# A four-layer graph network on one core: other preparation, other order of work, the edge maximum subtracted on TensorE and the sums inverted on ScalarE

## The reference, cut to what matters

```python
m     = segment_max(logits, dst)                 # one maximum for each target and head
ex    = exp(logits - m[dst])
denom = segment_sum(ex, dst)
out   = segment_sum(x_src_projected * (ex / denom[dst]), dst)
```

## Time and profile before

| what | us |
|---|---|
| median of 3 runs (4057.2 to 4076.98) | 4066.97 |
| the profiled execution, its own time | 4061.93 |
| the profiled execution, span of its instructions | 4060.2 |
| `prepare` | 0 to 68 |
| `node_pass` | 68 to 1232 |
| pass "0" and `source_columns` | 1232 to 1836 |
| pass "1" | 1836 to 2397 |
| pass "2a" | 2397 to 2945 |
| pass "2b" | 2945 to 3470 |
| pass "3" | 3470 to 4060.2 |

### The profile page before, as it was taken

The page is one execution under the profiler, slowest core; times in us unless marked ns, Lnnn a source line. Parts: engine busy times, 40 slices in busy tenths (PEclk is TensorE's granted clock), DMA queues, the critical chain, the costliest instruction groups (busy, mean ns, idle before and its releaser), DMA issues. The chain is left out here.

```text
span 4060.2 us, 72393 instructions
## 1 busy us (share of the span) xinstructions
PE 3500.2 (86%) x19961; PEld 2510.3 (62%) x20169; DVE 3558.8 (88%) x6756; ACT 2879.2 (71%) x9715; POOL 2308.0 (57%) x2305
## 2 busy tenths in 40 slices
PE   2999999999987999986999969999867777687775
PEld 2888888888864777764666645555534444354443
DVE  3899999999986999976999959999979999698786
ACT  2999999999975888875988855555546766344343
POOL 1577777777766777754433323345153442687777
PEclk9999999999988999998999989999989999898888
DMA  1455555555544343324544425555345554454442
GB/s 49 129 149 152 151 152 150 152 152 150 152 140 110 103 105 100 102 61 121 129 126 125 119 75 134 139 137 136 95 127 146 143 147 127 129 133 119 114 117 67
DMA packets 719120, 503.45 MB, mean 124 GB/s; under 512 B 141745, under 2 KB 621335, under 8 KB 718960
## 3 DMA queue, kind: packets, MB, share of 16 engines
q1 hardware_dynamic: 533072, 362.39, 33.0%
q0 software_dynamic: 56528, 81.64, 7.6%
q10 hardware_dynamic: 129360, 57.82, 5.1%
HBM read 304.28 MB, written 200.10 MB: 124 GB/s over the span
## 5 line engine op out<-in xcount | busy, mean ns | idle before, releaser
L1169 POOL DMA_INDIRECT slot_src_rows<-x,src_table_cols x392 | 420.7, 1073 | 453.1 <-PE psum L226 227.4
L237 ACT ACTIVATE node_z<-psum 128x128 f32<-128x128 f32 x1568 | 419.8, 325 | 22.5 <-PE psum L217 14.7
L1169 POOL DMA_INDIRECT slot2a_src_rows<-x,src_table_cols x196 | 220.5, 1125 | 335.0 <-PE psum L226 201.3
L646 ACT ACT_TABLE_LOAD x306 | 392.6, 1283 | 12.9 <-issue 7.7
L237 ACT ACTIVATION_READ_ACCUMULATOR node_z<-psum 128x1 f32 x1568 | 348.5, 227 | 0.0
L237 ACT ACTIVATE slot_logit<-psum 128x128 f32<-128x128 f32 x980 | 256.8, 279 | 125.9 <-PE psum L1337 99.8
L1169 POOL DMA_INDIRECT slot2b_src_rows<-xl,src_table_cols x196 | 198.2, 1011 | 257.1 <-PE psum L226 210.5
L1194 POOL DMA_INDIRECT out_nodes<-slot_new,out_index x196 | 243.0, 1240 | 59.8 <-issue 58.9
L1001 POOL DMA_INDIRECT node_gathered<-in_x,src_cols x196 | 235.8, 1203 | 47.0 <-issue 47.0
L1173 POOL DMA_INDIRECT slot_dst_rows<-in_x,dst_gather_cols x196 | 211.0, 1076 | 84.4 <-issue 50.9
L1166 POOL DMA_INDIRECT map_cols<-slot_map,src_cols x196 | 213.6, 1090 | 59.7 <-issue 59.7
(11 more groups left out here) (417 smaller groups left out, 12180.5 us busy)
## 6 DMA issues: line engine op xcount, KB each, us to landing
x<-node_x SPq DMA_DIRECT2D x294, 256.0 KB, 2.9
slot_neg<-neg SPq DMA_DIRECT2D x147, 256.0 KB, 4.5
node_xT<-in_x_T SPq DMA_DIRECT2D x98, 256.0 KB, 3.1
out_nodes<-node_x SPq DMA_DIRECT2D x98, 256.0 KB, 2.8
x<-slot_new ACTq DMA_DIRECT2D x98, 256.0 KB, 2.3
slot_keep<-keep SPq DMA_DIRECT2D x98, 256.0 KB, 4.2
slot_dst_rows<-x SPq DMA_DIRECT2D x98, 256.0 KB, 5.4
xl<-node_xl SPq DMA_DIRECT2D x98, 128.0 KB, 2.9
```

The lines of the kernel that those rows point to most:

```text
L237: ins = act.activation(g.z[u][:, t, :], rows[:, t, :], ACT.Square, scale=float(D ** -0.5), accum_out=sums[u][:, t:t + 1])
L646: act.add_instruction(mybir.InstLoadActFuncSet(name=nc.get_next_instruction_name(), ins=[], outs=[], act_func_set_id=wanted[0]))
L1169: pool.indirect_dma_start(src_rows[u][:, t, 0:src_width], None, table, column(c.src_table_cols[order], u, i, t))\
```

## The change

It touches `prepare`, `pe_rows`, the chains and steps of passes "0", "1", "2a" and "2b", the lookups of `slot_map`, and all five lists of `PLAN`.

- **`prepare`**: 60 loads in place of 62, in three groups with semaphores of their own, 33 issued by SyncE and 27 by ScalarE; work starts as its group arrives. The bias parts are made from columns by two small matmuls and one copy, where each was made from rows in 36 copies and 12 subtractions. After the wait for the last group VectorE has 39 instructions.
- **`pe_rows`**: the bias matmul reads 15 partitions (`level_of`, `bias_levels`), over the same columns.
- **"0", "1", "2a"**: `tot`, `rec`, `rs` and `rB` go. ScalarE takes the logarithm (`ln`) and the exponential of its negative (`inv`) of the whole 128x512 tile of sums in SBUF, and `agg` reads that. In "1" and "2a" VectorE first adds the two parts of the sum (`tot`, 128x512).
- **"1", "2a", "2b"**: `e_p` moves to TensorE, which adds `-I` times `fmax` to the logits in PSUM; ScalarE's `exp` is parted in `exp_p` (from PSUM) and `exp` (SBUF), 128x512 each.
- **"2a" and "2b"**: the leaky ReLU is made of a ReLU and a linear part, each with its own product, so VectorE's `z` goes. In "2a" the values are copied to `val` by ScalarE (`v`), which `pv` reads.
- **Lookups**: pass "0" makes 116 of the 196 (three for a chunk), pass "1" the others, two for a chunk; `source_columns` comes after "1".
- **`PLAN`**: new start times for every edge pass, on the same period; the lists of numbers are left out here.

```diff
 def pe_rows(pe, g, u, bank, parts, bias=None, width=P):
-        pe.matmul(bank(u)[:, 0:TILES * width], g.c.ones[:, 0:P], bias[:, 0:TILES * width], start=True, stop=False)
+        levels = tiles_of(g.c.bias_levels[:, :])[:, :, 0:width]
+        pe.matmul(bank(u)[:, 0:TILES * width].rearrange("p (t n) -> p t n", t=TILES), g.c.level_of[:, ROW_BIASES.index(bias), :], levels,
+                  start=True, stop=False)
...
+    by_sp = loads["rows"] + loads["first"][0::2] + loads["late"][0::2]
+    by_act = loads["first"][1::2] + loads["late"][1::2]
...
+        @block.scalar
+        def _(act):
+            with nc.allow_non_contiguous_dma("a few vectors"):
+                for item in by_act:
+                    act.dma_start(*item).then_inc(arrived[group_of[id(item)]], 16)
...
-        "2a": [("DVE", "dst"), ("PE", "z"), ("PE", "zo"), ("ACT", "z"), ("ACT", "zo"), ("DVE", "z"),
-               ("PE", "r"), ("PE", "v")],
-        "2b": [("DVE", "dst"), ("PE", "z"), ("ACT", "z"), ("DVE", "z"), ("PE", "r")],
+        "2a": [("PE", "v"), ("ACT", "v"), ("DVE", "dst"), ("PE", "z"), ("PE", "zo"), ("ACT", "z"), ("ACT", "zo"),
+               ("PE", "r"), ("PE", "o")],
+        "2b": [("DVE", "dst"), ("PE", "z"), ("ACT", "z"), ("ACT", "zl"), ("PE", "r")],
...
     softmax = [("DVE", "fc"), ("DVE", "f"), ("DVE", "shift"), ("DVE", "e_p"), ("DVE", "e_c"), ("ACT", "exp")]
+    if layer in ("1", "2a", "2b"):
+        softmax = [("DVE", "fc"), ("DVE", "f"), ("PE", "e_p"), ("DVE", "shift"), ("DVE", "e_c"), ("ACT", "exp_p"), ("ACT", "exp")]
     if layer == "0":
-        sums = [("DVE", "v"), ("DVE", "den"), ("DVE", "pv"), ("PE", "tot"), ("DVE", "num"), ("DVE", "tot")]
+        sums = [("DVE", "v"), ("DVE", "den"), ("DVE", "pv"), ("ACT", "ln"), ("DVE", "num"), ("ACT", "inv"), ("DVE", "agg")]
     elif layer == "1":
-        sums = [("ACT", "exps"), ("PE", "o"), ("DVE", "den"), ("DVE", "pv"), ("PE", "tot"), ("DVE", "num"), ("DVE", "sv"), ("DVE", "ns"), ("DVE", "tot")]
+        sums = [("ACT", "exps"), ("PE", "o"), ("DVE", "den"), ("DVE", "pv"), ("DVE", "num"), ("DVE", "sv"), ("DVE", "tot"), ("ACT", "ln"),
+                ("DVE", "ns"), ("ACT", "inv"), ("DVE", "agg")]
...
     mean = [("DVE", "rec")] + ([] if layer == "2b" else [("ACT", "rs")]) + [("PE", "rB"), ("DVE", "agg")]
+    if layer in ("0", "1", "2a"):
+        mean = []
...
     if layer == "0":
-        side += [("POOL", f"dst_gather{t}") for t in range(TILES)]
+        side = [("POOL", f"gather{t}") for t in range(3)] + [("POOL", f"dst_gather{t}") for t in range(TILES)]
+    elif layer == "1":
+        side += [("POOL", "gather_row0"), ("POOL", "gather_row1")]
...
+                elif step == "exp_p":
+                    act.wait_ge(*g.PE.done(u, i, "e_p"))
+                    act_copy(act, g, u, expo[u][:, 0, :], (A if layer == "2a" else B)(u), ACT.Exp)
+                elif step == "exp" and layer in ("1", "2a", "2b"):
+                    act.wait_ge(*g.DVE.done(u, i, "e_c"))
+                    act_copy(act, g, u, expo[u][:, 1, :], expo[u][:, 1, :], ACT.Exp)
...
+                elif step == "ln" and layer in ("1", "2a"):
+                    act.wait_ge(*g.DVE.done(u, i, "tot"))
+                    act_copy(act, g, u, expo[u][:, 2, :], expo[u][:, 2, :], ACT.Ln)
+                elif step == "ln":
+                    act.wait_ge(*g.DVE.done(u, i, "den"))
+                    act_copy(act, g, u, expo[u][:, 2, :], den[u][:, :], ACT.Ln, c.tiny[:, 0:1])
+                elif step == "inv":
+                    act.wait_ge(*g.ACT.done(u, i, "ln"))
+                    act_copy(act, g, u, expo[u][:, 2, :], expo[u][:, 2, :], ACT.Exp, scale=-1.0)
...
                 elif step == "r" and layer == "2a":
+                    pe.wait_ge(*g.ACT.done(u, i, "z"))
+                    pe.matmul(A(u), c.src_linear[:, :], src, start=True, stop=False)
+                    pe.matmul(A(u), c.own_linear[:, :], dst, start=False, stop=False)
+                    pe.matmul(A(u), c.src_relu[:, :], first, start=False, stop=False)
                     pe.wait_ge(*g.ACT.done(u, i, "zo"))
-                    pe.matmul(A(u), c.own_rows[:, 0:D], c.ones[:, :], start=True, stop=False)
...
+                elif step == "e_p":
+
+                    pe.wait_ge(*g.DVE.done(u, i, "f"))
+                    pe.matmul((A if layer == "2a" else B)(u), c.minus_ident[:, :], fmax[u][:, 1:CHUNK + 1], start=False, stop=True,
+                              skip_group_check=True).then_inc(g.pe_out[u], 1)
...
                 elif step == "r":
-                    pe.wait_ge(*g.DVE.done(u, i, "z"))
-                    product(u, B, [(c.pair_gap[:, :], first)])
+                    pe.wait_ge(*g.ACT.done(u, i, "z"))
+                    pe.matmul(B(u), c.pair_relu[:, :], first, start=True, stop=False)
+                    pe.wait_ge(*g.ACT.done(u, i, "zl"))
+                    pe.matmul(B(u), c.pair_linear[:, :], second, start=False, stop=True).then_inc(g.pe_out[u], 1)
...
+                elif step == "tot" and layer in ("1", "2a"):
+                    after("den")
+                    after("sv")
+                    ins = v.tensor_tensor(expo[u][:, 2, :], den[u][:, :], expo[u][:, 2, :], ALU.add)
...
+                elif step == "agg" and layer in ("0", "1", "2a"):
+                    after("ns" if own else "num")
+                    v.wait_ge(*g.ACT.done(u, i, "inv"))
+                    ins = v.tensor_tensor(agg[u][:, :], (t2 if own else num)[u][:, :], expo[u][:, 2, :], ALU.mult)
```

More of the change, by code:

```diff
@@ L190 @@
 UNCOUNTED = ("store", "gather", "put", "dst_gather", "scatter")
+ROW_BIASES = ("b1", "b2", "bias", "bl2", "xlr")
+LEVELS = 3 * len(ROW_BIASES)
 def tiles_of(t):
@@ L288, in sb, with fetch, load, column @@
         return ctx.enter_context(nc.sbuf_tensor(name, shape, dt))
-    loads = []
-    def load(name, shape, src, dt=F32, room=None):
+    loads = {"rows": [], "first": [], "late": []}
+    def fetch(into, src, group):
+        loads[group].append((into, src))
+    def load(name, shape, src, dt=F32, room=None, group="late"):
         t = (room or sb)(name, shape, dt)
-        loads.append((t[:], src))
+        fetch(t[:], src, group)
         return t
[L297 to L301, removed]
+    def column(name, src, m=P, group="late"):
+        return load(name, [m, 1], src.rearrange("(p o) -> p o", o=1), group=group)
     own = ExitStack()
@@ L365, in prepare @@
     c.payload = sb("payload", [P, SLOT_TILES, 2], I32)
[L368 to L379, removed]
+    row_here = [load(f"row_here{o}", [SLOT_CHUNKS, CHUNK], a["dst_rows"][o], I32, temp, "rows") for o in range(2)]
+    row_prev = [load(f"row_prev{o}", [SLOT_CHUNKS, CHUNK], a["dst_prev_rows"][o], I32, temp, "rows") for o in range(2)]
+    raw = {n: load("raw_" + n, [P, D], src, room=temp, group="first") for n, src in (
+        ("W1b", a["L0_gnn_W1"][D:2 * D, :]), ("W2", a["L0_gnn_W2"]), ("W1a", a["L0_gnn_W1"][0:D, :]))}
+    raw_cols, wide_bl2 = temp("raw_cols", [P, 3]), temp("wide_bl2", [P, 1])
+    for k, src in enumerate((a["L0_gnn_b1"], a["L0_gnn_b2"], a["L1_gnn_bias"])):
+        fetch(raw_cols[:, k:k + 1], src.rearrange("(p o) -> p o", o=1), "first")
+    fetch(wide_bl2[0:C2, :], a["L2_gnn_bl2"].rearrange("(p o) -> p o", o=1), "first")
+    raw_blin = load("raw_blin", [P, D], a["L2_gnn_blin"].partition_broadcast(P), room=temp, group="first")
+    br1 = load("br1", [P, 1], a["L2_gnn_br1"].rearrange("(p o) -> p o", o=1), room=temp, group="first")
+    here = [load(f"here{o}", [P, SLOT_TILES], a["dst_cols"][o], I32, temp) for o in range(2)]
+    after = [load(f"after{o}", [P, SLOT_TILES], a["dst_next_cols"][o], I32, temp) for o in range(2)]
     vectors = {}
@@ L423, in _ @@
             with nc.allow_non_contiguous_dma("a few vectors"):
-                for dst, src in loads:
-                    sp.dma_start(dst, src).then_inc(loaded, 16)
+                for item in by_sp:
+                    sp.dma_start(*item).then_inc(arrived[group_of[id(item)]], 16)
             sp.wait_ge(masks, 4)
@@ new lines, in _ @@
+            v.wait_ge(worked, n)
+            for k in range(len(to_center)):
+                n = did(v.bn_aggr(mean[:, k, :], stats[:, k, :]))
+            v.wait_ge(worked, bias1_at)
+            did(v.tensor_scalar(c.value_bias1[:, :], c.node_bias1[:, :], 1.0, None, ALU.add))
+            v.wait_ge(sums_ready, 1)
+            did(v.tensor_copy(biases[:, 0:3], psum[:, 6, D:D + 3]))
+            did(v.tensor_copy(biases[:, 3:4], wide_bl2[:, :]))
+            biases_at = did(v.tensor_tensor(biases[:, 4:5], wide_bl2[:, :], psum[:, 6, 0:1], ALU.subtract))
@@ new lines, in _ @@
+            did(v.scalar_tensor_tensor(out=c.Wlin1[C2:C2 + 1, :], in0=raw_blin[C2:C2 + 1, :], scalar=1.0,
+                                       in1=psum[C2:C2 + 1, 7, 0:D], op0=ALU.add, op1=ALU.subtract))
+            v.wait_ge(worked, n)
+            for k, (source, out) in enumerate(to_center[0:2]):
```

(27 more changed lines are left out.)

470 lines of the change are left out of this document (243 added, 227 removed), and 50 rows, old and new, of the table PLAN.

## The result

The kernel after takes 4045.07 us (median of 5 runs, 4041.57 to 4049.15), the kernel before in the same job 4069.0 (5 runs, 4057.2 to 4076.98): a ratio of 0.9945, with a 95% interval of 0.9926 to 0.9965. It is faster, by about 0.5%, where 4% were forecast; 3904 and the range of 3855 to 3985 were wrong. The profiled execution has a span of 4043.4 us.

What follows compares the result with a forecast made beforehand. One full engine bounds each edge pass (TensorE, VectorE or GpSimd); preparation is serial. -34 - 43 - 5 - 33 - 48 = -163 from 4061.9 gives 3899, plus 5 for the median: 3904 us, range 3855 to 3985.

Steps and rivals of the forecast that it cites:

- Bias rows: Bias matmuls, node pass included: the bf16 matmul streams the same 512 columns, so 0.21 us as before, change 0.
- Preparation: Start of the kernel: fewer loads on SyncE and a shorter VectorE tail start nodes at 33 instead of 68, -34 us.
- "0", 10.58: Pass "0": TensorE loses the transposes `tot` and `rB`, pace 11.45 to 10.58 us a chunk, -43 us.
- B: Rival, pass "0": GpSimd becomes the bound if all seven issues are long, +54 us, so 3958; chance 0.06.
- The rule against the change: Pass "0": two-SBUF-input VectorE instructions contend with GpSimd, so `agg` and `tot` would lengthen issues and "0" lose its gain.
- "1", 10.35: Pass "1": pace 10.45 to 10.35 us a chunk, between ends 10.20 and 11.08; -5 us, between -12 and +31.
- A: Rival, passes "0" and "1": ScalarE becomes the bound, +17 and +36 us, so 3957; chance 0.18.
- "2a", 9.81: Pass "2a": pace 10.48 to TensorE's 9.81 us a chunk, -33 us; chain of `v` and `z` on bank `A` costed 0.
- "2b", 8.9: Pass "2b": VectorE loses `z` and `e_p`, TensorE gains two products; pace 9.89 to 8.9, -48 us, between -25 and -59.
- "3", 0 within 19: Pass "3": same instructions in another order, 0; a fifth more or fewer long GpSimd issues would be 19 us either way.
- C: Rival, "1", "2a", "2b": TensorE stands at `e_p` waiting for the scan `f`, +296 us, so 4200; chance 0.03.
- Clock: TensorE's granted clock: all four changed passes above 88% busy, so no change of it was priced.

Runs made afterwards that it cites:

- the reverse edit in before: The kernel before with its bias matmuls reading 32 partitions in place of 128: 4210.23 us, ratio 1.0347.
- the 128-row kernel: The kernel after with the bias levels and their selecting weights padded with zeros from 15 to 128 partitions: 3894.38 us, ratio 0.9575 to before.

## Why the prediction was wrong

- **Bias rows, costed at 0: this step failed.** It counted the 512 columns, which are the same, and overlooked the rows, which are not: 0.30 us a bias row between 128-row products, 588 of them, 176 us in all. Undoing it is worth 150.7 us in the medians (4045.07 to 3894.38), more than the 141 us to the forecast (not all 176, as TensorE is no longer full everywhere then: 891.81 of 900 us in the node pass); the reverse edit in before costs 144, 16 of them in "2b", where no bias row is. The new operand was in the diff, and no rival doubted it.
- **Preparation, -34: right, near its end.** The first node product starts at 31.2 for 71.3, -40. (From 68 to 33 would have been -35, not -34.) TensorE then waits 5.62 us for `node_xT`, no longer for VectorE.
- **"0", 10.58: right once the rows are 128**, at 10.76 inside the 2% that were allowed; TensorE is busy 340.32 of 344.18 us there. B didn't come: GpSimd's mean in "0" of after is (144.5 + 88.1) / 217 = 1.07, with 128 rows 1.12. The rule against the change was not put to the test by `agg`: in the steady stretch of "0" no issue begins in it, in either of the two kernels.
- **"1", 10.35: nearly right.** 10.43 with 128 rows; VectorE is the bound (332.52 of 333.87 us) and ScalarE, at 307.86, is not, so A falls. VectorE's sum was 0.2 a chunk short; the scan `dst`, for one, 1.10 from start to start before, takes 1.19.
- **"2a", 9.81: the pace was there to be had, but the chain was costed at 0.** The moved `v` stood behind two DMA issues on ScalarE, which the prediction had not counted on its queue: 0.5 us a chunk.
- **"2b", 8.9: mis-sized.** 9.20, -37 for -48 and inside its bounds; no engine is full (TensorE 284.61 and VectorE 287.80 of 294.41 us).
- **"3", 0 within 19: mis-sized.** -43. The bound supposed that a fifth of the long issues at most could change, and that a long one takes 1.41. In before 40 of 243 took over 1.7 us; in after 6 of 240 do. (The product of the bound is 18, not 19.)
- **C didn't come.** No wait of TensorE in the steady stretches of the three passes names `e_p`'s scan.
- **Clock, priced at no change: right in the four changed passes**, at 1.00; in "3" it rose from 0.89 to 0.96.

That the 128-row kernel landed 10 us from 3904 is partly luck: "3" gave 43 more than forecast, and "1", "2a" and "2b" together 38 less.

## What to carry to other kernels

Compare the partitions of a small matmul's operands with its neighbours', not only its columns: between 128-row products, pad a short contraction with zeros to 65 rows or more, or put the short ones side by side (tried here with two equal ones). When a step is moved to another engine, look at which DMA issues stand ahead of it in that queue. Where GpSimd issues without a gap, moving its issues against VectorE's steps with two SBUF inputs can be worth a per cent without changing any instruction.

## What was not expected of the hardware

- A bf16 row of 15, 32 or 64 partitions between 128-row products takes 0.30 us more, 0.10 each for the instruction ahead, itself and the one behind; one of 65 or 128 takes none.
- Two 15-row matmuls in a row start 0.23 us apart, so the second is hardly dearer than its columns.
- A GpSimd DMA issue that begins 0.1 to 0.8 us into a VectorE scan with two SBUF inputs ends about 0.8 us behind the scan, wherever it begins (1.90 and 1.28 us); one that begins before the scan, or in a scan that reads PSUM, is not lengthened (0.94 to 1.02).
